# A cross-attention and FFN kernel on one core: the products of a projection unit moved from four score chunks of a loop step to the last three

## The reference, cut to what matters

```
x + attention(layernorm(x), ctx)             # x: 1600 tokens x 512; ctx: 5776 keys x 512
    q = (x @ Wq + bq) / sqrt(32)             # 16 heads of 32
    k, v = ctx @ Wkv + bkv
    q, k, v = fq_sym(q), fq_sym(k), fq_sym(v)    # q, k per row of a head; v per column over all keys
    p = fq_unsigned(softmax(q @ k.T))            # 255 levels per row
    out = (p @ v) @ Wp + bp
x + ffn(layernorm(x))                        # 512 -> 2 x 1408 -> 512, int8-like inputs to each product
```

## Time and profile before

| | us |
|---|---|
| median of 3 runs | 1858.56 |
| lowest and highest | 1850.79 and 1858.99 |
| span of the profiled execution | 1854.7 |

### The profile page before, as it was taken

The page is one execution under the profiler, slowest core; times in us unless marked ns, Lnnn a source line. Parts: engine busy times, 40 slices in busy tenths (PEclk is TensorE's granted clock), DMA queues, the critical chain, the costliest instruction groups (busy, mean ns, idle before and its releaser), DMA issues.

```text
span 1854.7 us, 42223 instructions
## 1 busy us (share of the span) xinstructions
PE 1634.9 (88%) x17032; PEld 1158.1 (62%) x17032; DVE 1691.6 (91%) x2670; ACT 1391.8 (75%) x1362; POOL 1429.3 (77%) x1159
## 2 busy tenths in 40 slices
PE   7997889888888888888888888887889988789998
PEld 6884666666565666655666666554555555478876
DVE  6868999989999999999999999998999999986665
ACT  2446899888988888989888888888788888842232
POOL 1432889889988898999898999898899899753232
PEclk9999999998999999989999999999999999889999
DMA  5578998899899988898999998889988998742221
GB/s 172 194 222 201 194 200 177 173 182 179 168 178 192 195 180 183 176 183 168 187 189 189 186 179 177 169 142 186 174 172 161 194 188 163 167 127 45 66 58 47
DMA packets 851533, 309.98 MB, mean 167 GB/s; under 512 B 784966, under 2 KB 813964, under 8 KB 851212
## 3 DMA queue, kind: packets, MB, share of 16 engines
q1 hardware_dynamic: 851340, 307.29, 80.6%
HBM read 74.26 MB, written 39.59 MB: 61 GB/s over the span
## 4 chain that ended last, share of the span: by engine, by line
DVE 44%; PE 20%; POOL 14%; issue 8%; DMA 7%; ACT 6%; SPq 1%; POOLq 0%; DVEq 0%; ACTq 0%
DVE S L1279 40%; POOL PT L1501 11%; PE PS L867 5%; DMA PP<-Pr 5%; ACT Pr L1074 4%; PE PK L904 3%; PE PS L702 2%; PE PK L673 2%; PE PS L734 2%; PE PK L675 1%; PE PO L675 1%; PE PO L673 1%; DVE MJ L1305 1%; DVE VMX L1174 1%; POOL VB L1449 1%
## 5 line engine op out<-in xcount | busy, mean ns | idle before, releaser
L1279 DVE TENSOR_SCALAR_CACHE_REDUCE S<-PS,SQN 128x1536 f32<-128x1536 f32 (+1 forms) x768 | 1284.2, 1714 | 28.1 <-PE PS L734 22.6
L1501 POOL CAST PT<-PP 128x1536 uint16<-128x1536 uint8 (+1 forms) x800 | 1099.6, 1419 | 112.5 <-DMA PP<-Pr 110.8
L1074 ACT ACTIVATE Pr<-S,MS 128x5888 uint8<-128x5888 f32 x200 | 1041.3, 5206 | 170.5 <-DVE MJ L1305 138.4
L734 PE MATMUL PS<-KT,QT 96*128 96x512 bf16 (+1 forms) x2496 | 635.7, 374 | 133.9 <-DVE S L1279 120.4
L753 PEld LDWEIGHTS PO<-VI,PT 128*128 128x128 f16 x9200 | 339.7, 96 | 190.1 <-POOL PT L1501 21.8
L734 PEld LDWEIGHTS PS<-KT,QT 96*128 96x128 bf16 (+1 forms) x2496 | 198.6, 99 | 341.7 <-issue 132.9
L753 PE MATMUL PO<-VI,PT 128*128 128x32 bf16 x9200 | 356.5, 178 | 11.6 <-ACT AO L1028 7.3
L673 PE MATMUL PK<-WG,CT 128*128 128x128 f32 (+1 forms) x1288 | 215.3, 297 | 42.4 <-ACT VV L940 39.8
L675 PE MATMUL PK<-CT,WG 128*128 128x128 f32 (+1 forms) x1288 | 213.3, 295 | 5.5 <-DMA CT<-ctxt 5.5
L673 PEld LDWEIGHTS PK<-WG,CT 128*128 128x128 f32 (+1 forms) x1288 | 170.0, 195 | 49.2 <-issue 48.2
L675 PEld LDWEIGHTS PK<-CT,WG 128*128 128x128 f32 x1288 | 168.4, 194 | 7.0 <-issue 5.7
(11 more groups left out here) (156 smaller groups left out, 1556.6 us busy)
## 6 DMA issues: line engine op xcount, KB each, us to landing
CT<-ctxt SPq DMA_DIRECT2D x180, 256.0 KB, 3.2
k_rows<-KS SPq DMA_DIRECT2D x39, 512.0 KB, 4.0
q_rows<-QS SPq DMA_DIRECT2D x13, 512.0 KB, 4.7
W13F<-w13T SPq DMA_DIRECT2D x12, 352.0 KB, 3.7
PP<-Pr SPq DMA_TRANSPOSE x200, 5.9
XT<-x SPq DMA_DIRECT2D x12, 256.0 KB, 4.3
XR<-x SPq DMA_DIRECT2D x12, 256.0 KB, 3.3
base_rows<-XO SPq DMA_DIRECT2D x12, 256.0 KB, 3.3
```

The source lines that it names most:

```text
L734: last = pe.matmul(PS[n % 2][p0:p0 + r, f:f + w], QT[h % 3][0:PARTS * HD, q0:q0 + r], KT[h % 3][0:PARTS * HD, c * CHUNK + f:c * CHUNK + f ...
L1074: act.activation(Pr[i % 2].rearrange("p t q b -> p t b q"), S[i % 2].rearrange("p (t b q) -> p t b q", b=2, q=P), ACT.Exp, bias=MS[:, i % ...
L1279: v.tensor_scalar(S[i % 2][:, c * CHUNK:c * CHUNK + CW[c]], PS[n % 2][:, 0:CW[c]], neg_step, None, ALU.mult, ALU.min, accum_out=MN[:, i % ...
L1501: gp.tensor_copy(PT[i % 2][:, 2 * t0:2 * t1, :].rearrange("p (t b) q -> p t b q", b=2), PP[i % 2][:, t0:t1, :].bitcast(U8).rearrange("p t ...
```

## The change

A unit's eight products are numbered as eight pieces, 0 to 3 for the keys and 4 to 7 for the values. A table `UNIT_PART` gives the pieces a chunk takes: none behind chunk 0, pieces 0 to 2 behind chunk 1, 3 to 5 behind chunk 2, 6 and 7 behind chunk 3. With two units in a step, chunk 1 takes six pieces of the first unit, chunk 2 its last two and four of the second, chunk 3 the last four of the second. The number of products, their operands and their order among themselves are as before.

```diff
+UNIT_PART = (0, 0, 3, 6, 2 * NK)
...
-            def unit(g, u, slices=range(NK)):
+            def unit(g, u, pieces=range(2 * NK)):
...
-                if 0 in slices:
+                if 0 in pieces:
                     pe.wait_ge(s_ct[k % RING], 16 * (k // RING + 1))
...
-                for c in (2, 3, 0, 1) if k == 0 else slices:
-                    for d in range(2 * (c % 2), 2 * (c % 2) + 2):
-                        if c < 2:
-                            pe.matmul(bank[0:n, 0:GC], CT[k % RING][:, d, 0:n], WG[:, d, 0, :], start=(d == 0), stop=False)
-                        else:
-                            last = pe.matmul(bank[:, GC:GC + n], WG[:, d, 1, :], CT[k % RING][:, d, 0:n],
-                                             start=(d == 0), stop=(d == NK - 1))
-                    if c == 1:
+                for piece in (4, 5, 6, 7, 0, 1, 2, 3) if k == 0 else pieces:
+                    d = piece % NK
+                    if piece < NK:
+                        pe.matmul(bank[0:n, 0:GC], CT[k % RING][:, d, 0:n], WG[:, d, 0, :], start=(d == 0), stop=False)
+                    else:
+                        last = pe.matmul(bank[:, GC:GC + n], WG[:, d, 1, :], CT[k % RING][:, d, 0:n],
+                                         start=(d == 0), stop=(d == NK - 1))
+                    if piece == NK - 1:
...
-                if NK - 1 in slices:
+                if 2 * NK - 1 in pieces:
                     last.then_inc(M["s_ku"], 1)
...
-                    work = [(unit_, k) for unit_ in units for k in range(NK)]
-                    for unit_, k in work[c * len(units):(c + 1) * len(units)]:
-                        unit(*unit_, [k])
+                    work = [(unit_, piece) for unit_ in units for piece in range(2 * NK)]
+                    for unit_, piece in work[UNIT_PART[c] * len(units):UNIT_PART[c + 1] * len(units)]:
+                        unit(*unit_, [piece])
```

## The result

| | median us | runs |
|---|---|---|
| before | 1855.45 (1849.57 to 1861.00) | 20 |
| changed | 1849.84 (1844.71 to 1857.15) | 20 |

The ratio is 0.9971, 95% interval 0.9959 to 0.9982: faster by 0.29%, 5.4 us. The time forecast was 1849.9 us. The gain forecast was 8.7 us, from a median before of 1858.56 us that 20 runs put at 1855.45. So that the time was met to 0.1 us is luck, two errors cancel: the gain was too large by 3 us, and the starting point was too high by 3 us. Of the three outcomes that were given chances the likeliest came, within 0.5% (0.51); the gain itself lies just under the forecast's 5.5 to 12.5 us, at the edge to the first rival's 2 to 5. In a run whose time and span are both known the time is 1.8 us above the span (1846.16 and 1844.4), not 3.9.

The account below looks back on a forecast made before the run. DVE, busy 97% of the loop, was taken as the bound, with 23.5 us of waits for PE's scores as ceiling. -13.7 + 1.0 + 2.5 + 1.5 = -8.7 us gave 1849.9 us, range 1846 to 1853.

Parts of the forecast that it names:

- three outcomes: Chances for the measured time: faster by over 0.5% 0.42, within 0.5% 0.51, slower by over 0.5% 0.07.
- first rival: DVE's waits turn into waits for the exponential, transposing DMA and POOL; gain only 2 to 5 us, 1855 us; chance 0.22.
- The place of the wait: PE meets its wait for ACT behind chunk 1's scores, not before them; these waits fall from 39.8 to under 10 us.
- The 13.7 us removed: DVE's long waits for scores at seven places, 15.08 us in sum, less 1.1 and 0.25 us that remain.
- (a): Seven steps with two units, more products behind chunks 1 and 2: DVE waits longer, +1.0 us, bounds -1 and +3.5.
- (b): PE's idle time is placed elsewhere, giving a few new low-clock stretches: three taken, +2.5 us.
- seven places: Steps 29, 35, 48, 54, 87, 98 and 104: PE waits for ACT, then chunk 1's scores are late; 15.08 us.
- Step 29: PE first waits for ACT's read of PO, which is untouched; about 1.1 of DVE's 3.33 us were to remain.
- second rival: Idle stretches in 36 batch steps lower PE's clock, 0.8 us each, 29 us in all: 1875 us, slower; chance 0.09.
- Its counter-argument: PE already waited for ACT nearly there, 0.66 us in the mean; such waits lowered no clock unless about 1 us or longer.
- (c): Where DVE no longer waits for scores it can meet a late exponential: +1.5 us, bounds 0 and +6.
- The rows that were to show it: Profile after: DVE's waits for scores 9 to 13 us, for the exponential about 6, one wait each for seven two-unit pairs.

Follow-up runs that it names:

- e1_again: The changed kernel once more with no edit, for a second profile; ratio to before 0.9966, 1851.26 us.
- e3_light_after: The changed kernel with a quarter of the bytes in the transposes of the values of groups 1 to 3; ratio to before 0.9953.

## Why the prediction came out as it did

**The place of the wait**: right. PE waits 3.7 us for ACT at the unit, forecast under 10; without the removal of the wait (one piece back) most of the gain is gone.

**The 13.7 us removed**: right in kind, too large as a typical value. Net of the new costs (a) and (b) the wait for scores was to fall by 13.7 - 1.0 - 2.5 = 10.2 us. In the first pair of profiles it fell by 23.5 - 10.0 = 13.5 us. Over the four profiles of each kind in the table the means are 19.95 and 10.70: 9.3 us, near the 10.2. That is partly luck again. The list of long waits was read from one execution with the clock low at all seven places; in the second one of before the same seven come to 7.6 us where they came to 15.08, and a new one at step 76 adds 2.2. And at steps 54 and 104 the wait for scores went but one for the exponential took its place. Step 29 was to keep 1.1 us and step 98 0.1 to 0.25: nothing stood there in the first profile, 0.78 + 0.37 + 1.01 and 1.50 + 0.54 in the second.

**(a) Two-unit steps**, +1.0 us: the mechanism and the seven steps were right, the pair of waits is as forecast (one before the last chunk, one at the next step). The size is next to nothing: seven times 0.57 is 4.0 us, and the same seven pairs came to 3.95 us before (the second of a pair was 0.18 to 0.47). The run with the old partition shows why: the new partition of the two-unit steps costs 1.7 us, and the second waits, which the one-unit steps behind them no longer have, give 1.6 back. Chunk 2 grew by 0.45 us, as reckoned (0.4); but chunk 1 was through earlier than reckoned: the scores of chunk 2 start 236.00 - 233.59 = 2.41 us after DVE's chunk 0, before 239.56 - 237.00 = 2.56.

**(b) New low-clock stretches**, +2.5 us: few. The first profile has low stretches in steps 34, 54 and 104 among the steps with units, the second in 28, 34, 53, 98 and 104; before had seven. Step 34 is new in both and costs about 1.0 us at its chunk 2, behind a wait of 0.9 us for the exponential. Forecast were three to six places; the second rival, a low stretch at every one of the 36 batch steps, is out. Its counter-argument, that only waits of about 1 us or more lower the clock, fits the first profile of before and not the second, where waits of PE for ACT of 1.44, 1.30 and 1.17 us leave it at its upper level.

**(c) Give-back to the exponential**: this is the step that failed. It was put at 1.5 us, with 0 to 6 as bounds. The means of the table go from 3.9 to 8.8 us, +4.9, and ACT's own wait for the transposing DMA from 30.5 to 47.7. So (c) was 4.9 us and not 1.5, and this term alone is as much as the 3 us by which the gain was too large. The first rival, the gain given back downstream, was half true. In sum the waits go from 23.8 to 19.5 us, -4.3, beside a measured -5.4 us; the 1.1 us between them isn't accounted for. (Four of the eight profiles are of kernels with a small cut; without them the sums are 24.0 and 20.3. Single profiles scatter as much as the effect: the first pair fell by 8.6 us, the second rose by 1.1.)

What makes the exponential late can be read in the trace for the three largest places (54, 104, 154): SP issues the transposes of queries, keys and values ahead of that of the probabilities. The run that moved the values' ones doesn't prove it, as said there. At step 34 it is something else. There SP itself waits for POOL's unpacking before it can issue the transpose of step 30, for which the exponential of step 32 then waits 4.75 us and DVE at step 34 0.90. SP's wait between 390 and 400 us of the changed kernel's first profile:

```profile
SPq L620 <- POOL PT L1502: 5.4, 1, 5.4
```

POOL has the key quantisation (L1431, L1434, L1439) and L1477 ahead of that unpacking, from 387.3 to 392.6 us. For the small waits it isn't known. The two cuts that were to double the gain left it at 0.31 and 0.33%, so neither the values' bytes nor POOL's widening of the values is the main thing that limits it.

**The rows that were to show it**: pairs at steps 10/11, 20/21, 30/31, 60/61, 75/76, 110/111 and 125/126 are there, all seven, 0.24 + 0.33; DVE's waits for scores 10.0 in the forecast 9 to 13, but 15.8 over the same stretch of the second profile, still under the 18 that would have refuted it; waits for the exponential 8.0 and 9.7, above the 6.

## What to carry to other kernels

On an engine that runs in order, look at what stands behind a wait, not at how long the wait is: 40 us of waits at PE cost DVE about 20, and putting the critical work (the next scores) ahead of the wait gave back half of that, though PE's work stayed and ACT is still late. Before a gain is summed from the long waits of one trace, profile the same kernel twice and look at the granted clock behind each wait; here the second profile alone moves the sum by 4 us. And when the bound engine's stalls are taken out, look for what the next ring (here exponential, DMA, unpacking) takes back; here it was about half of the fall in the means, and from under a third to more than all of it in single pairs of profiles.

## What the runs showed of the hardware

The times of one kernel spread over some 10 us, and this goes with PE's mean granted clock in the same run. In the 29 runs of the kernel before beside e1_again, the time falls by 1.0 us for each 0.001 of mean clock, correlation -0.73; the changed kernel's first profile had 0.982 and 1846.16 us, its second 0.977 and 1855.61. Which of the two drives the other isn't shown by that. The mean clock of the two kernels there is almost the same (0.9782 and 0.9789); at that slope it stands for 0.7 us of the 6 between them.

Much the same wait of PE, 0.97 to 1.59 us, is followed by the lower clock in one execution and by the upper one in another (steps 35, 48 and 87 in the two profiles of the kernel before).

Issuing a transposing DMA holds SP for long: between 515 and 560 us of the changed kernel's first profile 3.6 to 4.8 us for the probabilities and 1.2 to 1.9 us for each of the smaller ones, against 0.58 us at most for a plain load. Where five DMAs stand ahead of the probabilities', in loop steps of about 7 us, SP's issue time decides when that one can start. A quarter of the bytes hardly shortens the issue: in e3_light_after a transpose of values takes SP 1.12 and 1.18 us in the same steps, 1.20 and 1.19 uncut.
